# A recommendation tower on one core: the MLP's matmuls between the gram matmuls instead of between the lookups, and row transposes spread over a step

## What is computed

```python
e = jnp.stack([tbl_0[ids[:, 0]], ..., tbl_25[ids[:, 25]]], axis=1)      # 2048 x 26 x 128
sd = jnp.einsum('bfd,bd->bf', e, x)
ss = jnp.einsum('bfd,bgd->bfg', e, e)
pairs = ss[:, iu, ju]                                                    # upper triangle, 325
h = jnp.concatenate([x, sd, pairs, x], axis=1)
h = jnp.maximum(h @ W_top1 + b_top1, 0.0)                                # 607 -> 512
h = jnp.maximum(h @ W_top2 + b_top2, 0.0)                                # 512 -> 256
y = h @ W_top3                                                           # 256 -> 1
```

## Time and profile before

| | |
|---|---|
| median of three runs | 551.03 us (550.11 to 553.82) |
| the profiled execution, its own time | 554.1 us |
| its span | 552.2 us |
| TensorE matmuls busy | 375.6 us, 68% |
| TensorE weight loads busy | 294.6 us, 53% |
| GpSimd busy | 277.3 us, 50% |
| VectorE busy | 231.4 us, 42% |
| ScalarE busy | 174.7 us, 32% |
| TensorE's mean granted clock | 0.805 |
| chain that ended last | PE 62%, issue 21%, ACT 7% |

### The profile page before, as it was taken

One profiled execution on the slowest core, in us unless ns is written; L12 is line 12 of the kernel. 1 busy time (PEld: TensorE's weight loads), 2 busy tenths in 40 slices (PEclk: granted clock), 3 DMA queues, 4 the chain that ended last, 5 costly groups with the idle time before them and its releaser, 6 DMA issues.

```text
span 552.2 us, 12229 instructions
## 1 busy us (share of the span) xinstructions
PE 375.6 (68%) x5424; PEld 294.6 (53%) x5424; DVE 231.4 (42%) x579; ACT 174.7 (32%) x221; POOL 277.3 (50%) x297
## 2 busy tenths in 40 slices
PE   2650587426379959955489859954559859975697
PEld 0430455315267648745367647743448648864576
DVE  5610687414144553532244443632226535505500
ACT  1400345313132343421142333421215324443122
POOL 7777467563416656753516756663416666610000
PEclk9985599667579979976579969965569978996699
DMA  8522263110102112211101112211101111100000
GB/s 201 142 53 52 67 198 89 40 49 23 40 8 53 44 38 53 66 35 37 40 10 52 44 38 52 63 43 30 27 20 40 43 43 49 43 18 4 4 0 1
DMA packets 11596, 26.93 MB, mean 49 GB/s; under 512 B 5033, under 2 KB 5161, under 8 KB 11409
## 3 DMA queue, kind: packets, MB, share of 16 engines
q0 software_dynamic: 9216, 18.89, 13.4%
q1 hardware_dynamic: 2328, 7.27, 4.9%
HBM read 26.14 MB, written 0.01 MB: 47 GB/s over the span
## 4 chain that ended last, share of the span: by engine, by line
PE 62%; issue 21%; ACT 7%; another core or an unknown queue 7%; DMA 2%; POOL 1%; DVE 1%
PE sum_bank L410 22%; PE vec_bank L436 12%; PE work_bank L462 8%; PE vec_bank L426 6%; PE work_bank L472 5%; ACT vecT L316 3%; PE work_bank L458 3%; PE work_bank L481 2%; ACT vecT L310 2%; PE work_bank L450 2%; PE id_bank L396 1%; DMA rows<-in_tbl,ids_all 1%; ACT parts L296 1%; ACT late L342 1%
## 5 line engine op out<-in xcount | busy, mean ns | idle before, releaser
L221 POOL DMA_INDIRECT rows<-in_tbl,ids_all x288 | 274.6, 953 | 207.7 <-PE vec_bank L426 86.5
L253 DVE TENSOR_TENSOR onehot<-id_bank,row_f 125x1024 fp32r<-125x1024 f32 x128 | 151.6, 1220 | 170.6 <-PE sum_bank L410 72.8
L410 PE MATMUL sum_bank<-onehot,parts 125*128 125x512 f32 x512 | 166.0, 459 | 4.2 <-DVE onehot L253 4.2
L436 PE MATMUL vec_bank<-vecT 128*26 128x26 f32 x4096 | 68.7, 215 | 81.4 <-issue 73.7
L410 PEld LDWEIGHTS sum_bank<-onehot,parts 125*128 125x128 f32 x512 | 103.1, 213 | 30.8 <-issue 12.2
L316 ACT COPY vecT<-vec_bank 128x512 f32<-128x512 f32 x72 | 85.3, 1200 | 80.7 <-remote 49.0
L436 PEld LDWEIGHTS vec_bank<-vecT 128*26 128x26 f32 x4096 | 56.4, 131 | 96.4 <-issue 85.0
L264 DVE STREAM_TRANSPOSE late<-late 128x832 f32<-128x832 f32 x16 | 28.7, 1793 | 113.6 <-ACT late L325 113.6
L426 PE MATMUL vec_bank<-ident,rows 128*128 128x128 f32 x288 | 52.1, 314 | 10.6 <-DMA rows<-in_tbl,ids_all 3.8
L325 ACT COPY late<-vec_bank 128x416 f32<-128x416 f32 x32 | 16.2, 507 | 123.1 <-PE vec_bank L436 123.1
L426 PEld LDWEIGHTS vec_bank<-ident,rows 128*128 128x128 f32 x288 | 41.2, 162 | 23.9 <-issue 11.7
(11 more groups left out here) (23 smaller groups left out, 99.2 us busy)
## 6 DMA issues: line engine op xcount, KB each, us to landing
rows<-in_tbl,ids_all POOLq DMA_INDIRECT x288
late<-in_tbl SPq DMA_DIRECT2D x8, 480.0 KB
w_all<-in_weights SPq DMA_DIRECT2D x1, 1540.0 KB
xT<-in_dense_t SPq DMA_DIRECT2D x4, 256.0 KB
late<-in_weights SPq DMA_DIRECT2D x1, 256.0 KB
ids_all<-in_ids SPq DMA_DIRECT2D x1, 208.0 KB, 3.0
late<-in_tbl SPq DMA_DIRECT2D x8, 20.0 KB
vecT<-in_ids_t SPq DMA_DIRECT2D x1, 64.0 KB
```

The lines of the kernel that those rows point to most:

```text
L221: nc.gpsimd.indirect_dma_start(rows[:, g % ROWS_RING, n, t, :], None, tables[f], bass.IndirectOffsetOnAxis(ids_all[:, TD * d + t, f:f + 1], 0)
L253: nc.vector.tensor_tensor(onehot[:, use % RING, :, :], bass.AP(got.tensor, got.offset, [got.ap[0], [0, PW], [1, QS]]), bass.AP(numbers.ten ...
L410: last = nc.tensor.matmul(sum_bank[into % 2][:], parts[:, part, CH_AT[n] + c0 + c, :], onehot[:, use % RING, c, :], start=(p % PER == 0 an ...
L436: last = nc.tensor.matmul(vec_bank[into % 2][BL * j:BL * j + GC, i * GC:(i + 1) * GC], vecT[:, s, 0:GC], vecT[:, s, 1:VECS], start=True, s ...
```

## The change

Five things are changed.

1. The MLP of quad q-1 leaves the lookups of quad q. Its layers 1 and 2 now stand between the gram matmuls of quad q: a half tile's 64 gram matmuls are cut into eight chunks of eight, and behind a chunk stands at most one MLP matmul (`LAYER1_AT`, `LAYER2_AT`). Halves 0 to 3 carry the first duo, halves 4 to 7 the second; 24 matmuls a duo. Layer 3 follows half 3 and half 7, and the pair transposes of tiles 2 and 3 follow half 3. Those of tiles 0 and 1 stand behind packs 1 and 3. The tail has the last quad's MLP as before, now with all of its pair transposes.
2. Row transposes: in quads 1 to 3 nine groups stand between the packs, from pack 3 on and every third or fourth, and in quad 0 thirteen. In the grams a group follows each of halves 0 to 2, two follow half 3, and the first four groups of the next quad (`EARLY`) follow halves 4 to 7.
3. VectorE's turns stand behind packs 5 (two), 8 and 11.
4. Layer 3 has the weight column as stationary operand and 256 moving columns, and gives one output row, in two matmuls a duo.
5. The results stand in two rows of the tile that holds the ids in fp16 (`lines`), and two DMAs store them.

The head and the places where the order is set:

```diff
-    ROWS_IN_A = 15
+    EARLY = 4
+    ROWS_IN_A = 9
     ROWS_AFTER = {}
     for j in range(ROWS_IN_A):
-        ROWS_AFTER.setdefault(max(j, 31 - 5 * (ROWS_IN_A - 1 - j) // 2), []).append(j)
-    ROWS_AFTER_GRAM = {0: [15], 1: [16, 17]}
-    TURN_AFTER = {RING - 1: [0, 1, 2], RING + 1: [3]}
-    PAIRS_AFTER_GRAM = {2: 0, 3: 1}
...
-    LAYER3_AFTER = {13: 0, 29: 1}
-    PAIRS_AFTER = {14: 2, 15: 3}
+        ROWS_AFTER.setdefault(min(PACKS - 1, 3 + 7 * j // 2), []).append(EARLY + j)
+    ROWS_AT_FIRST = {}
+    for j in range(EARLY + ROWS_IN_A):
+        ROWS_AT_FIRST.setdefault(min(PACKS - 1, 3 + 3 * j), []).append(j)
+    ROWS_AFTER_HALF = {0: [13], 1: [14], 2: [15], 3: [16, 17]}
+    NEXT_AFTER_HALF = {4: 0, 5: 1, 6: 2, 7: 3}
+    TURN_AFTER = {RING - 1: [0, 1], RING + 2: [2], RING + 5: [3]}
+    PAIRS_AFTER = {1: 0, 3: 1}
+
+    CHUNKS = 8
...
             def gram(q, t, h):
                 into = gram_at(q, t, h)
                 free_vec(into)
-                for i in range(HALF):
-                    for j in range(4):
-                        s = t * P + BL * j + h * HALF + i
-                        last = nc.tensor.matmul(vec_bank[into % 2][BL * j:BL * j + GC, i * GC:(i + 1) * GC],
-                                                vecT[:, s, 0:GC], vecT[:, s, 1:VECS], start=True, stop=True)
-                last.then_inc(vec_filled, 1)
+                for c in range(CHUNKS):
+                    for i in range(HALF * c // CHUNKS, HALF * (c + 1) // CHUNKS):
+                        for j in range(4):
+                            s = t * P + BL * j + h * HALF + i
+                            last = nc.tensor.matmul(vec_bank[into % 2][BL * j:BL * j + GC, i * GC:(i + 1) * GC],
+                                                    vecT[:, s, 0:GC], vecT[:, s, 1:VECS], start=True, stop=True)
+                    if c == CHUNKS - 1:
+                        last.then_inc(vec_filled, 1)
+                    if q:
+                        layers(2 * (q - 1) + t // TD, (2 * t + h) % TQ, c)
...
             def layer3(d):
                 use = NW * d + W3
                 pe.wait_ge(work_drained, use)
-                for t in range(TD):
-                    for b in range(M2):
-                        last = nc.tensor.matmul(work_bank[use % 2][:, t:t + 1], h2[:, b, t * P:(t + 1) * P],
-                                                w3_sb[:, b:b + 1], start=(b == 0), stop=(b == M2 - 1))
+                for b in range(M2):
+                    last = nc.tensor.matmul(work_bank[use % 2][0:1, 0:DS], w3_sb[:, b:b + 1], h2[:, b, :],
+                                            start=(b == 0), stop=(b == M2 - 1))
                 last.then_inc(work_filled, 1)
...
                     if q:
-                        mlp(q - 1, p)
+                    if q and p in PAIRS_AFTER:
+                        transpose_pairs(q - 1, PAIRS_AFTER[p])
...
+                for half in range(2 * TQ):
+                    if half == TQ:
                         pe.wait_ge(vec_drained, rows_at(q, 2 * GROUPS - 1) + 1)
-                    for h in range(2):
-                        gram(q, t, h)
-                    for j in ROWS_AFTER_GRAM.get(t, []):
+                    gram(q, half // 2, half % 2)
+                    for j in ROWS_AFTER_HALF.get(half, []):
                         transpose_rows(q, j)
-                    if t in PAIRS_AFTER_GRAM:
-                        transpose_pairs(q, PAIRS_AFTER_GRAM[t])
-            for p in range(PACKS):
-                mlp(QUADS - 1, p)
+                    if half in NEXT_AFTER_HALF and q + 1 < QUADS:
+                        transpose_rows(q + 1, NEXT_AFTER_HALF[half])
+                    if q and half % TQ == TQ - 1:
+                        layer3(2 * (q - 1) + half // TQ)
+                    if q and half == TQ - 1:
+                        for t in range(TD, TQ):
+                            transpose_pairs(q - 1, t)
```

143 lines of the change are left out of this document (81 added, 62 removed).

## The result

| | before | after |
|---|---|---|
| median of four runs each, side by side | 552.42 us | 612.14 us |
| the profiled execution, its own time | 554.1 us | 612.02 us |
| its span | 552.2 us | 610.2 us |
| mean granted TensorE clock | 0.805 | 0.809 |

The changed kernel takes 1.1075 times as long, 95% interval 1.1008 to 1.1143. The forecast was slower, at 571 us; the time lies above its range, 496 to 598 us, and at the figure of rival C, 613 us.

The account below looks back on a forecast made before the run. It took gathers and dense streams of small products to exclude one another in a single chain. From the 552.2 us span, - 87 + 17.5 + 39 + 32 + 18 + 0.5 gave 572, less 1.2: 571 us, range 496 to 598.

Parts of the forecast that it names:

- rival C: Second and third grams: nothing of the inserted MLP is hidden, 21 us more in each, 613 us in all; chance 0.09.
- Lookups of steps 2 to 4: With MLP and six row groups gone, these stages take 53 us each, a gain of 87 us in all.
- over 65 us: Sign of being wrong: lookups this long mean the MLP there only lay in time spent waiting for gathers.
- First lookups and first gram: First step: lookups unchanged at 111 us, gram 67 us instead of 49.5, a loss of 17.5.
- The term of the spread rows: First three grams: each of eight halves beside its own four gathers takes 7.0 us, 67 us a gram without MLP.
- Second and third gram: With spread rows and a third of 32 us of MLP exposed, 78 us each, losses of 39 and 32.
- An inserted product: An MLP product between gram chunks costs 0.67 us, 0.43 itself and 0.24 for changing width; 32 us a step.
- Fourth gram: No gathers beside it, so bound by execution: 48 us instead of 29.7, loss 18, ends 44 and 62.
- Here the idle time really is filled: Claim for the gram without gathers: MLP products fill TensorE's idle time, giving 48 us; 62 if nothing is filled.
- Tail: Last MLP and result stores: moved pair transposes, shorter layer 3 and two DMAs lose 0.5 us, ends -1 and +3.
- Rival A: Grams of steps 2 to 4: MLP products remove the stops, each costs what the fourth does; 495 us, chance 0.20.
- Rival B: First three grams: a stop costs by the gather, not the half; first gram 56 us, 538 in all; chance 0.27 with surroundings.

Follow-up runs that it names:

- mlp_only_5: Changed kernel with row transposes where the kernel before has them, MLP still between gram products; 621.37 us beside 553.74 for the kernel before, 1.1257.
- rows_only_3: Kernel before with only the row transposes spread as in the change, MLP still in the lookups; 566.68 us beside 553.22 for the kernel before, 1.025.
- after_again: Changed kernel, unchanged, run again where the kernel before takes about 552 us; 612.58 us, 1.1066 of the kernel before.
- before_again: Kernel before, unchanged, run again in the slow condition to have its trace; 551.67 us, 0.9973.
- after_third: Changed kernel, unchanged, run again in the fast condition; 449.83 us beside 433.21 for the kernel before, 1.0367.
- grouped form: Changed kernel with all MLP products of a half tile behind its last chunk; 625.09 us, 1.1277 of the kernel before, and 625.21 us, 1.1308.

## Why the prediction was right on the sign and wrong on the size

By stages, my values against those of the profiled execution: first lookups 111 and 94.5; first gram 67 and 79.8; lookups of steps 2 to 4 53 each and 55.7, 53.5, 50.5; second and third gram 78 each and 92.3, 93.5; fourth 48 and 55.9; tail 32.3 and 34.4. The differences sum to +37, of which the second to fourth gram have 38.

*Lookups of steps 2 to 4: right in size, wrong in cause.* I had a gain of 87 us, and it is 88. That the number fits is luck. I worked the 87 from TensorE's work that leaves, 18.6 + 3.7 us of MLP and 2.6 of row groups a step, since I took TensorE to lead there. With stops, mlp_only_5 gains 14 us over three steps by taking the MLP out, and rows_only_3 54 us by taking six groups of gathers out. Only behind that is the MLP's leaving worth something, 13 us a step (196.2 to 157.1 us over three, rows_only_3 to after_again). The lookups had waited for gathers. The condition "over 65 us" that I named for this case was met by mlp_only_5 and not by the change, since the change moved both.

*First lookups and first gram: the sum right, the split wrong.* Together they take 174.3 us where I had 178. I took the lookups as 0 since their long stop lay beside gathers into free buffers. It is 16 us shorter, and the gathers not done there, 16 in a row from 90.4 to 110.1, stand beside the first half of the gram, which takes 18.9 us; the halves behind it take the 7.8 us that I had put (7.0 + 0.7). The term of the spread rows, 8 x 7.0, holds: rows_only_3 has 66.6 and 66.5 us in the second and third gram, where I had 67 for a gram with no MLP.

*Second and third gram: the step that failed.* The prediction said "I take a third as exposed, 11 us", of 32. In after_again the two grams are 26 and 27 us longer than in rows_only_3, and so is the fourth (56.0 against 28.9), though no gathers stand beside it. With no stops the same MLP adds 23 and 24 us (52.6 against 29.2 and 28.4). So the stop hides nothing of it on balance: 29.2 us of gram, 37.4 us of stops (66.6 less 29.2) and 23.4 us of MLP are 90 of the 92.5. My argument was that half of a half's products stand ahead of the stop, at the price of 0.67 us. Some idle time was filled: from rows_only_3 to after TensorE's idle time falls by 13 and 10 us in the second and third gram, and its busy time rises by 39 and 37. What the sum had at nothing is the clock. The product takes 1.15 us and not 0.63 at 1.2 GHz, and with 26 and 20 products there this is 13 and 10 us, so by this working the clock took back what interleaving filled. It is the larger part of what I missed, but no run holds the clock fixed, and it is not all: in mlp_only_5 only 10 and 12 products run at the low level, 5 and 7 us, and its second and third gram are 26 and 33 us longer than those of before_again even so. The earlier trace rows had the sign of the clock, 0.57 to 0.65 in grams. I used it only as a point for rival C and gave C 0.09. That the time meets C's 613 us is in part luck: C had 99 us for these two grams, which took 92 and 94, and 48 for the fourth, which took 56.

*An inserted product* was put at 0.67 us and its chunk at 0.16. Measured at 2.4 GHz they are 0.63 and 0.23, 0.86 together against 0.83. *Fourth gram*: I had 48 us, and it took 56. 64 chunks at up to 0.23 are 14 to 15 us where I had 10; the rest of the difference I haven't split. "Here the idle time really is filled" holds for some 7 us: a product with its chunk adds 0.86 less the 0.16 of a chunk before, 0.7 us, and 28.9 + 48 x 0.7 is 62.5. The ends that I gave, 44 and 62, held it. *Tail*: +2.6 us for +0.5.

*What the change costs, part by part.* With stops the rows cost +13.5 us, the MLP +68, and both +59 to +60. They don't add: spreading the gathers saves 8 us once the MLP is in the grams. The main cost is the MLP's move. It is taken from a place where it cost 13 us a step and put where it costs 26 to 27. Without any gather the sum is the same in kind, 18 to 21 us out of the lookups and 22 to 26 into the grams, +12 in all. Without stops but with gathers the parts are -4 to -8 for the rows, +25 to +31 for the MLP and +16.6 for both, and there the gathers set the pace: only the fourth gram, behind the last of them, carries its MLP in full. No version here beat the kernel before in both conditions. The rows alone were 1 to 2% below it without stops, and 2.5% above it with them.

*Rival A* has each gram of steps 2 to 4 cost what the fourth does. With stops it is refuted, 92.5 and 93.6 us against 56.0. Without stops it is what is seen (52.6, 52.6 and 50.3 us at clock 1.00), and the change is slower than before even so, since the kernel before has no stops to lose there either. The Trainium skill, "Perfetto Trace Analysis", Optimization Strategy, says that interleaving regimes in which another engine is the most contended may help. It did not pay here: the work moved and the work it was put between are both TensorE's, which is busy 51.33 of 53 us with them in after_third, and the change, its MLP part or its grouped form was slower than before in each of the six groups. *Rival B* put a gram with the spread rows and no MLP at 56 us, and rows_only_3 has 66.6 and 66.5. Its price is refuted. That the cost goes by the gather is not: 37.7 us for 36 gathers (66.6 less 28.9) is 1.05 us each, just over the highest of the three ratios that I had, 1.0.

## What to carry to other kernels

Idle time between short products is not free room for larger ones. Ask which clock is granted there, and what the inserted instruction costs at that level, with its change of width in and out, against the same instruction where it stands now. Here the MLP and six row groups were put at 25 us of TensorE in the lookups (18.6 + 3.7 + 2.6), and without gathers they raised its busy time in a gram by 33 to 36 us and filled 10 to 12 us of idle time. When two engines wait for each other in a stage, the busy share tells which work can leave, but not what the stage waits for; take each piece out alone before crediting the stage's gain to it. Measure a change that depends on such waits more than once, at different times and beside the unchanged kernel, since that kernel's own time may not be the same each time.
